# Local attention: epsilon by a sum over two columns, parameters read in place, W1 at the step's begin and the GELU of two items ahead of the output product

## The chip, the cores and the metric

The kernel runs on one core of a Trainium2 chip. The metric is the device time of one launch in microseconds. The core's engines are called PE (matrix products), DVE (vector), ACT (activations), POOL (the second vector engine) and SP (which issues the DMAs here); each runs its own list of instructions in order, and they meet through semaphores.

## The reference, cut to what matters

Input are 16 items of 256 tokens with 128 channels. Three parts follow one another: a first attention, six layers of local attention with a feed-forward part, and a state space part. The change is in the six layers:

```
for i in range(6):
    x = attn_layer(shift_tokens(x), Wqkv[i], q_scale[i], k_scale[i], Wo[i]) + x
    x = ffn_layer(shift_tokens(x), ln_g[i], ln_b[i], W1[i], b1[i], W2[i], b2[i]) + x

def ffn_layer(x, g, bln, W1, b1, W2, b2):
    mu = x.mean(-1, keepdims=True)
    var = ((x - mu) ** 2).mean(-1, keepdims=True)
    xn = (x - mu) / jnp.sqrt(var + 1e-05) * g + bln
    a, gate = jnp.split(xn @ W1 + b1, 2, -1)
    return a * jax.nn.gelu(gate, approximate=False) @ W2 + b2
```

`attn_layer` has 16 heads of 64, a norm and a rotation of q and k, and a softmax over the own window of 32 keys and the one before. The inner width of the feed-forward part is 341, kept in three chunks of 128, 128 and 85 rows, each with a value half (`ha`) and a gate half (`hgate`).

## The kernel before, in words

`phase_b` takes 96 items (6 layers of 16) through a pipeline written out in Python: `phase_b_steps` calls each engine's `body` for steps n = -1 to 98. In step n the *front* works on item n+1 (projection, rotation, norm of q and k), the *attention* on item n, the *tail* on item n-1 (product with Wo, residual, layer norm), the *ffn* stage on item n-2 (product with W1, GELU) and the *closing* stage on item n-3 (gate times value, product with W2, residual). Layer and item are plain Python numbers, so nothing is looked up at run time.

A step has 32 slots. They are no times: every engine walks through slots 0 to 31 in order, and tables say in which slot it issues what. The order within one engine is therefore fixed by the tables, and between engines by semaphores alone.

- Scores of the attention's four rounds: slots 0, 8, 16, 24 (PE L1007, L1018, then DVE's row maximum L1349). Exponentials (ACT L1177) four and five slots later, eight instructions a round. DVE scales them (L1339, L1343) seven and eight slots after the scores. PE turns them (L1029) and ACT copies the turned ones (L1220) at eight and eleven. Values (PE L1044) at fourteen, their copy (ACT L1208) at fifteen. What reaches past slot 31 is done in the next step.
- Scores wait until the exponentials of the round before have read the banks.
- Projection pieces (PE L1063 to L1065) at slots 0, 2, 6, 8, 15, 16, 17, 21, 22, 24, 29, 30, in two banks by turns. A piece waits until the piece two before it has been read: by DVE's rotation (L1291, L1293) for q and k, by ACT's copy (L1201) for v. Squares are ACT L1197, their sums DVE L1295; POOL adds the rotated halves (L1380), clamps (L1382) and takes the power (L1384). The norm's product is POOL's (L1369) or DVE's (L1302, slots 27 and, late, 4).
- Two *spare* PSUM banks go round by turns among: the turned q/k tiles (PE L992, ACT copy L1147; slots 24, 26, 27, 28 and, late, 0, 4, 6, 7), the product with Wo (L1081, slots 11 and 12), the turned residual `xt` (L1088, slot 21), the turned layer norm `xn` (L1094, slot 31; ACT's copy with scale and bias L1159), W1's three chunks (L1121) and W2 (L1108, slot 29; read by DVE L1326, slot 31). A use waits until the use two before it has been read (`take_spare`).
- W1's chunk c, at slot s of `W1_SLOT`: PE L1121, then ACT reads the two halves with their biases (L1166 into `hgate`, L1167 into `ha`). Slots: chunk 0 at 5, chunk 2 at 17, chunk 1 at 21.
- The GELU (ACT L1224) is taken in odd steps only, over the gates of two items at once (128x1536), at slot 21, after that slot's exponentials. It needs another activation table than the exponential. POOL multiplies gate and value at slot 19 (L1390) and waits for the GELU's semaphore.
- Layer norm, DVE, slot 22 (`centred_stats`, L270): statistics (L273), `memset` of `var` to epsilon (L276), aggregation (L278), subtraction of the mean (L281), variance plus epsilon (L282). POOL takes the power and scales, slot 23 (`scaled_pool`, L288, L291).
- At the begin of each step DVE copies parameters into small tiles: ln scale and bias (L1266, `lnp`), b2 (L1270, `lend`), b2 and b1 (L1278, `lp`). ACT waits for them (`lnp_ready`, `lp_ready`), DVE for `lp_ready` before L1326.
- In the last step before a layer and in its first one ACT and DVE convert the layer's projection weights, with four of the six conversions at slots 1, 4, 7 and 10.

Of the kernel before, what the change touches and what calls it, by code (L numbers as in the profile page):

```python
# [726 lines left out]
W1_SLOT = {5: 0, 17: 2, 21: 1}  # L727
# [10 lines left out]
GELU_SLOT, RSTD_SLOT, GATE_SLOT = 21, 23, 19  # L738
# [99 lines left out]
def phase_b(nc, g, d, ps):  # L838
    with ExitStack() as stack:
# [389 lines left out]
        def _(dve):  # L1229
            for buffer in (s.xhi, s.xlo):  # L1230
                nc.vector.memset(buffer[:].bitcast(F32), 0.0)
            for buffer in (s.xs2, s.ha, s.V):
# [17 lines left out]
            def body(step):  # L1250
# [6 lines left out]
                def known(value):  # L1257
                    return value if isinstance(value, int) else dve.snap(value)

                if step.front is not None:  # L1260
                    lf = known(step.front[0])
                    next_src = known((step.front[1] + 1) % NB * NT)
                if step.tail is not None:
                    lt, dst = known(step.tail[0]), known(step.tail[1] * NT)
                    x_lower, x_upper, x_all = g.xT[lower, bass.ds(dst, NT)], g.xT[upper, bass.ds(dst, NT - 1)], g.xT[:, bass.ds(dst, NT)]
                    nc.vector.tensor_scalar_mul(s.lnp[:, step.odd], g.lparam[:, bass.ds(lt, 1), 0:2].rearrange("p a k -> p (a k)"), 1.0).then_inc(s.lnp_ready, 1)  # L1266
                if step.closing is not None:
                    lw, end = known(step.closing[0]), known(step.closing[1] * NT)
# [2 lines left out]
                    if step.ffn is None:
                        kept.then_inc(s.lp_ready, 1)
                if step.ffn is not None:
                    lu = known(step.ffn[0])
# [597 lines left out]
```

## Time and profile before

| | us |
|---|---|
| median of 3 runs | 4741.89 (4740.1 to 4744.51) |
| profiled execution | 4741.16 |
| its span, first to last instruction | 4739.4 |
| mean granted PE clock in it | 0.964 |
| local attention (`phase_b`) | some 500 to 4020 us of the span |

Times in the rows below are from the span's start. In timelines the first column is the start, the second the duration in us (merged over xN like instructions), and the bracket at the end is the idle time of the engine before it and who ended that. `b_`, `all_` and `until_b_` in front of a tile's name tell where it was allocated.

### The profile page before, as it was taken

The page shows a single profiled execution, that of the slowest core. Times are in us where ns is not written, and L with a number is a line of the kernel's source. Part 1 is how long each engine was busy: PE and PEld are TensorE (multiplying, and loading weights), DVE is VectorE, ACT ScalarE, POOL GpSimd, SP SyncE. Part 2 cuts the span into 40 slices and gives each one's busy share as a digit, 9 for nine tenths or more (in the row PEclk, how much of TensorE's full clock was granted, in tenths as well). Part 3 has the DMA queues.
Part 4 walks back from the last instruction along what each step waited for, and adds up shares of the span by engine and source line. Part 5 has one row for each costly group of instructions (what it writes and reads, how often), then busy time and mean ns, then how long its engine had stood idle before and what let it go on. Part 6 is the DMA issues. An engine that isn't in the chain of part 4 may idle for free. (4 is left out here: it accounts for less than half of the span.)

```text
span 4739.4 us, 124337 instructions
## 1 busy us (share of the span) xinstructions
PE 4228.0 (89%) x45166; PEld 3156.2 (67%) x45166; DVE 4078.0 (86%) x7658; ACT 3755.3 (79%) x11543; POOL 3540.7 (75%) x2504
## 2 busy tenths in 40 slices
PE   6898699999999999999999999999999997688887
PEld 3555477777777777777777777777777775445453
DVE  4776798989999999999999899999999995598887
ACT  2555588888888888888888888888888886777774
POOL 0010698999999899999999999999899994444444
PEclk9999799999999999999999999999999999788888
DMA  1000111112111121111111112111111111000000
GB/s 26 7 6 2 47 51 38 45 40 57 53 39 45 43 54 48 44 44 45 52 47 45 42 47 53 46 45 39 51 50 42 45 39 31 0 4 3 3 3 5
DMA packets 118569, 168.67 MB, mean 36 GB/s; under 512 B 26563, under 2 KB 44422, under 8 KB 118022
## 3 DMA queue, kind: packets, MB, share of 16 engines
q1 hardware_dynamic: 109246, 160.92, 12.8%
q8 instruction: 344, 5.64, 0.5%
q10 hardware_dynamic: 8776, 0.45, 0.1%
q14 instruction: 203, 1.66, 0.1%
HBM read 20.79 MB, written 2.10 MB: 5 GB/s over the span
## 5 line engine op out<-in xcount | busy, mean ns | idle before, releaser
L1380 POOL TENSOR_TENSOR b_w<-b_w,b_vt 128x512 f32<-128x512 f32 x768 | 1171.2, 1535 | 255.3 <-DVE b_vt L1293 145.3
L1384 POOL TENSOR_TENSOR b_rn<-b_ssm,all_neg_half 128x16 f32<-128x16 f32 x384 | 1219.2, 3175 | 32.0
L1177 ACT ACTIVATE b_Pr<-ps,b_nm 128x96 f32<-128x96 f32 x3072 | 1003.3, 354 | 0.6
L1177 ACT ACTIVATION_READ_ACCUMULATOR b_Pr<-ps,b_nm 128x1 f32 x3072 | 679.0, 221 | 0.0
L1220 ACT ACTIVATE b_PT<-ps 96x512 f32<-96x512 f32 x768 | 456.9, 595 | 240.3 <-PE ps L1029 227.4
L1063 PE MATMUL ps<-b_Whi,b_xlo 128*128 128x512 f32 x1152 | 579.5, 503 | 33.4 <-DVE b_vt L1293 18.5
L992 PE MATMUL ps<-all_ident,b_w 128*128 128x128 f32 x3072 | 467.9, 284 | 156.0 <-ACT b_qkT L1147 100.4
L1291 DVE TENSOR_TENSOR b_w<-ps,until_b_rotab 128x512 f32<-128x512 f32 x768 | 524.6, 683 | 60.5 <-ACT b_sq L1197 57.5
L1343 DVE TENSOR_TENSOR b_Pr<-b_Pr,b_rinv 128x384 f32<-128x384 f32 x768 | 534.7, 696 | 26.3
L1293 DVE TENSOR_TENSOR b_vt<-ps,until_b_rotab 128x512 f32<-128x512 f32 x768 | 523.0, 681 | 0.0
L1147 ACT ACTIVATE b_qkT<-ps 128x512 f32<-128x512 f32 x768 | 460.5, 613 | 76.6 <-PE ps L992 76.4
L1295 DVE TENSOR_REDUCE b_ss<-b_sq 128x8 f32<-128x512 f32 x768 | 519.5, 676 | 0.0
L1197 ACT ACTIVATE b_sq<-ps 128x512 f32<-128x512 f32 x768 | 476.0, 620 | 28.1 <-PE ps L1065 13.0
L1029 PE MATMUL ps<-all_ident,b_Pr 128*96 128x128 f32 x3072 | 478.5, 279 | 21.8 <-DVE b_Pr L1343 5.8
L992 PEld LDWEIGHTS ps<-all_ident,b_w 128*128 128x128 f32 x3072 | 343.6, 143 | 206.8 <-ACT b_qkT L1147 111.5
L1044 PEld LDWEIGHTS ps<-b_PT,b_V 96*64 96x64 f32 x12288 | 389.4, 138 | 137.4 <-issue 135.2
L1065 PE MATMUL ps<-b_Whi,b_xhi 128*128 128x512 f32 x1152 | 458.7, 398 | 0.0
L1064 PE MATMUL ps<-b_Wlo,b_xhi 128*128 128x512 f32 x1152 | 457.5, 397 | 0.0
L1044 PE MATMUL ps<-b_PT,b_V 96*64 96x64 f32 x12288 | 442.4, 225 | 1.2 <-ACT b_PT L1220 1.2
L1349 DVE TENSOR_REDUCE b_nm<-ps 128x8 f32<-128x768 f32 x384 | 367.5, 957 | 71.2 <-PE ps L1018 64.3
L1029 PEld LDWEIGHTS ps<-all_ident,b_Pr 128*96 128x96 f32 x3072 | 332.2, 127 | 121.5 <-issue 55.1
L1369 POOL TENSOR_TENSOR b_w<-b_w,b_rn 128x1024 f32<-128x1024 f32 x192 | 365.7, 1905 | 15.1
(259 smaller groups left out, 9461.0 us busy)
## 6 DMA issues: line engine op xcount, KB each, us to landing
b_V<-b_Vraw SPq DMA_DIRECT2D x384, 192.0 KB, 2.6
b_V<-b_Vraw SPq DMA_DIRECT2D x384, 128.0 KB, 2.4
b_V<-b_Vraw SPq DMA_DIRECT2D x192, 64.0 KB, 2.2
b_Wraw<-in_L_ffn_Wqkv SPq DMA_DIRECT2D x36, 256.0 KB, 3.4
b_Wo<-in_L_ffn_Wo SPq DMA_DIRECT2D x6, 512.0 KB, 4.1
a_xtok<-in_L_attn_hidden_states SPq DMA_DIRECT2D x16, 128.0 KB, 2.1
out<-c_xout SPq DMA_DIRECT2D x16, 128.0 KB, 1.8
b_W<-in_L_ffn_W SPq DMA_DIRECT2D x6, 341.0 KB, 3.7
```

Source lines behind the costliest of these rows:

```text
L992: last = nc.tensor.transpose(bank[:, i * P:(i + 1) * P], s.w[:, tt, c % 2, c // 2, i * P:(i + 1) * P], g.ident[:])
L1029: last = nc.tensor.transpose(ps[KEY_ROWS, T_BANK, (j * TT + tt) * P:(j * TT + tt + 1) * P], s.Pr[:, r % 2, j, a * TT + tt], g.ident[:])
L1044: last = nc.tensor.matmul(ps[j * DB:(j + 1) * DB, O_BANK, a * NT + blk * BLK:a * NT + (blk + 1) * BLK], s.V[KEY_ROWS, blk, head], s.PT[KEY ...
L1063: nc.tensor.matmul(ps[:, F_BANK[k % 2]], s.xlo[:, pf, rows], s.Whi[:, cols], start=True, stop=False)
L1177: last = nc.scalar.activation(s.Pr[:, r % 2, j, i], ps[:, S_BANK[j], i * KEYS:(i + 1) * KEYS], ACT.Exp, bias=s.nm[:, r, j, i:i + 1], accum ...
L1197: nc.scalar.activation(s.sq[:, i % 2], ps[:, F_BANK[k % 2]], ACT.Square).then_inc(s.act_front, 1)
L1291: nc.vector.tensor_tensor(s.w[:, tt, c % 2, which].rearrange("p (h e) -> p h e", e=DB), rotated, g.rotab[:, bass.ds(lf, 1), 2 * which, tt] ...
L1293: nc.vector.tensor_tensor(turned, raw[:, :, ::-1], sin.rearrange("p a (z e) -> p a z e", z=2).broadcast_to((P, 8, 2, DB // 2)), ALU.mult). ...
L1295: nc.vector.tensor_reduce(s.ss[:, j, which * 8:(which + 1) * 8], s.sq[:, i % 2].rearrange("p (h e) -> p h e", e=DB), AX.X, ALU.add).then_i ...
L1343: nc.vector.tensor_tensor(rows, rows, inverse, ALU.mult).then_inc(s.scaled, 1)
L1380: nc.gpsimd.tensor_tensor(rows, rows, s.vt[:, i % 4], ALU.add).then_inc(s.pool_add, 1)
L1384: nc.gpsimd.tensor_tensor(s.rn[:, j], s.ssm[:, j], g.neg_half[:, 0:HB], ALU.pow).then_inc(s.pool_r, 1)
```

## The change

Four edits, all in the local attention.

1. `ff`'s moment tile gets a third column that is set to epsilon once. Variance plus epsilon is a `tensor_reduce` over columns 1 and 2, in place of a `memset` and a `tensor_tensor`.
2. DVE's three parameter copies at the step's begin and their waits go; ACT and DVE read `g.lparam` in place.
3. W1's chunks 0, 1, 2 are at slots 1, 3, 5. The order of uses of the two spare banks follows from the slots, 15 uses a step as before.
4. The GELU is at slot 10, after the exponentials of slot 5 and before those of slot 12.

`bass.ds` of a Python number becomes a plain slice in the rotation, which is the same access.

```diff
+class CentredNorm(LayerNorm):
+    def __init__(self, s, name, xn):
+        super().__init__(s, name, xn)
+        self.mv = s.sb(name + "_mve", [P, TT, 3])
...
     dve.wait_ge(ln.moment, 2 * n + 1)
-    nc.vector.memset(ln.var[:], LN_EPS)
     for tt in range(TT):
-        last = nc.vector.bn_aggr(ln.mv[:, tt], ln.st[:, tt])
+        last = nc.vector.bn_aggr(ln.mv[:, tt, 0:2], ln.st[:, tt])
...
-    nc.vector.tensor_tensor(ln.var[:], ln.mv[:, :, 1], ln.var[:], ALU.add).then_inc(ln.var_ready, 1)
+    nc.vector.tensor_reduce(ln.var[:], ln.mv[:, :, 1:3], AX.X, ALU.add).then_inc(ln.var_ready, 1)
...
-W1_SLOT = {5: 0, 17: 2, 21: 1}
+W1_SLOT = {1: 0, 3: 1, 5: 2}
...
-GELU_SLOT, RSTD_SLOT, GATE_SLOT = 21, 23, 19
+GELU_SLOT, RSTD_SLOT, GATE_SLOT = 10, 23, 19
...
-                        act.wait_ge(s.lnp_ready, t + 1)
-                        nc.scalar.activation(s.xnT[:], ps[:, SPARE[bank], 0:NT], ACT.Identity, bias=s.lnp[:, pa, 1:2],
-                                             scale=s.lnp[:, pa, 0:1]).then_inc(s.spare_free[bank], 1)
+                        nc.scalar.activation(s.xnT[:], ps[:, SPARE[bank], 0:NT], ACT.Identity, bias=g.lparam[:, step.tail[0], 1:2],
+                                             scale=g.lparam[:, step.tail[0], 0:1]).then_inc(s.spare_free[bank], 1)
...
-                        act.wait_ge(s.lp_ready, u + 1)
...
+            nc.vector.memset(s.ff.mv[:], LN_EPS)
...
-                    nc.vector.tensor_scalar_mul(s.lnp[:, step.odd], g.lparam[:, bass.ds(lt, 1), 0:2].rearrange("p a k -> p (a k)"), 1.0).then_inc(s.lnp_ready, 1)
...
-                    kept = nc.vector.tensor_scalar_mul(s.lend[:], g.lparam[:, bass.ds(lw, 1), 2:3].rearrange("p a k -> p (a k)"), 1.0)
...
-                    if ("w1", 0) in step.uses_before:
-                        for b, uses in step.latest([("w1", c) for c in range(3)], True):
-                            dve.wait_ge(s.spare_free[b], uses + 1)
-                    nc.vector.tensor_scalar_mul(s.lp[:], g.lparam[:, bass.ds(lu, 1), 2:9].rearrange("p a k -> p (a k)"), 1.0).then_inc(s.lp_ready, 1)
...
-                            dve.wait_ge(s.lp_ready, u + 1)
-                            nc.vector.scalar_tensor_tensor(out=x_end, in0=ps[:, SPARE[b], 0:NT], scalar=s.lend[:], in1=x_end,
+                            nc.vector.scalar_tensor_tensor(out=x_end, in0=ps[:, SPARE[b], 0:NT], scalar=g.lparam[:, lw, 2:3], in1=x_end,
```

## Rows read from the trace of the kernel before

**Rows 1.** Busy time by windows: us, then PE, PEld, DVE, ACT, POOL busy, PEclk, DMA.

```profile
600.00:3990.00 3390.00, 3150.01 (x38588) 2509.12 (x38580) 3094.75 (x6031) 2977.62 (x9863) 3078.13 (x1963) 0.99 0.17 46
```

**Rows 2.** Timeline of DVE, steps 35, 41 and 42 (cut).

```profile
1796.14 1.25 DVE L1266 TENSOR_SCALAR b_lnp<-until_b_lparam 128x2 f32<-128x2 f32 x1
...
1833.75 0.16 DVE L1266 TENSOR_SCALAR b_lnp<-until_b_lparam 128x2 f32<-128x2 f32 x1
...
2011.77 1.25 DVE L1266 TENSOR_SCALAR b_lnp<-until_b_lparam 128x2 f32<-128x2 f32 x1
...
2020.90 0.17 DVE L1339 RECIPROCAL b_rinv<-b_ssum 128x4 f32<-128x4 f32 x1
...
2030.43 0.96 DVE L1349 TENSOR_REDUCE b_nm<-ps 128x8 f32<-128x768 f32 x1
...
2036.03 0.96 DVE L282 TENSOR_TENSOR b_ff_var<-b_ff_mv,b_ff_var 128x2 f32<-128x2 f32 x1
...
2038.90 0.96 DVE L1349 TENSOR_REDUCE b_nm<-ps 128x8 f32<-128x768 f32 x1 [0.41 <-PE ps L1018]
...
2048.28 0.16 DVE L1266 TENSOR_SCALAR b_lnp<-until_b_lparam 128x2 f32<-128x2 f32 x1
...
2067.32 0.96 DVE L1349 TENSOR_REDUCE b_nm<-ps 128x8 f32<-128x768 f32 x1
...
2075.80 0.96 DVE L1349 TENSOR_REDUCE b_nm<-ps 128x8 f32<-128x768 f32 x1 [0.41 <-PE ps L1018]
...
2083.05 1.25 DVE L1266 TENSOR_SCALAR b_lnp<-until_b_lparam 128x2 f32<-128x2 f32 x1
```

**Rows 3.** Timeline of ACT, step 41 (cut).

```profile
2020.06 0.63 ACT L1197 ACTIVATE b_sq<-ps 128x512 f32<-128x512 f32 x1
...
2025.07 0.59 ACT L1220 ACTIVATE b_PT<-ps 96x512 f32<-96x512 f32 x1 [1.57 <-PE ps L1029]
...
2028.78 0.60 ACT L1201 ACTIVATE b_Vraw<-ps 128x512 f32<-128x512 f32 x1 [0.56 <-PE ps L1065]
...
2037.70 1.28 ACT L1224 ACT_TABLE_LOAD   x1
2039.00 1.49 ACT L1224 ACTIVATE b_hgate<-b_hgate 128x1536 f32<-128x1536 f32 x1
2040.39 0.58 ACT L1197 ACTIVATE b_sq<-ps 128x512 f32<-128x512 f32 x1
```

**Rows 4.** Timeline of PE, step 41 (cut).

```profile
2016.08 1.03 PE L1121 MATMUL ps<-b_xnT,b_W 128*128 128x256 f32 x4
...
2019.58 1.06 PE L992 MATMUL ps<-all_ident,b_w 128*128 128x128 f32 x8 [0.69 <-DVE b_w L1302]
...
2037.83 0.36 PE L1007 MATMUL ps<-until_b_mask_bf,until_b_ident_bf 64*64 64x384 bf16 x4 [0.44 <-ACT b_Pr L1177]
...
2042.49 0.66 PE L992 MATMUL ps<-all_ident,b_w 128*128 128x128 f32 x4 [2.18 <-ACT b_qkT L1147]
```

**Rows 5.** Windows of the first and the last of 15 half-clock stretches (PEclk 0.50).

```profile
744.70:748.10 3.40, 3.40 (x11) 2.76 (x9) 2.15 (x3) 3.37 (x10) 3.40 (x3) 0.50 0.00 0
3700.70:3704.00 3.30, 3.28 (x14) 3.14 (x15) 3.30 (x5) 2.54 (x5) 3.22 (x4) 0.50 0.01 2
```

**Rows 6.** Lines of DVE: count, duration ns min/median/max, first and last start us, shapes.

```profile
L1266 DVE TENSOR_SCALAR b_lnp<-until_b_lparam x96: 156/184/1257, 575.3 to 3989.2; 128x2 f32<-128x2 f32 x96
L282 DVE TENSOR_TENSOR b_ff_var<-b_ff_mv,b_ff_var x96: 150/956/1084, 598.4 to 4000.6; 128x2 f32<-128x2 f32 x96
L1295 DVE TENSOR_REDUCE b_ss<-b_sq x768: 667/676/682, 514.0 to 3953.5; 128x8 f32<-128x512 f32 x192
L1343 DVE TENSOR_TENSOR b_Pr<-b_Pr,b_rinv x768: 557/559/1681, 548.1 to 3990.0; 128x384 f32<-128x384 f32 x192
```

**Rows 7.** Timeline of POOL, additions at the step's begin and at L282.

```profile
2009.18 3.81 POOL L1380 TENSOR_TENSOR b_w<-b_w,b_vt 128x512 f32<-128x512 f32 x2
...
2034.45 2.52 POOL L1380 TENSOR_TENSOR b_w<-b_w,b_vt 128x512 f32<-128x512 f32 x2
```

More of the change, by code:

```diff
@@ L855, in phase_b @@
         s.oT = s.sb("oT", [P, HPAIRS, NT])
-        s.lp = s.sb("lp", [P, 7]); s.lend = s.sb("lend", [P, 1]); s.lnp = s.sb("lnp", [P, 2, 2])
         s.xs2 = s.sb("xs2", [P, NT]); s.xtok = s.sb("xtok", [P, TT, P]); s.xnT = s.sb("xnT", [P, NT])
         s.ha = s.sb("ha", [P, 2, 3, NT]); s.hgate = s.sb("hgate", [P, 2, 3, NT])
-        s.ff = LayerNorm(s, "ff", s.xtok)
+        s.ff = CentredNorm(s, "ff", s.xtok)
         s.zeroed, s.wo_in, s.w1_in, s.w2_in, s.whi_done, s.w_ready = s.sems("zeroed wo_in w1_in w2_in whi_done w_ready")
@@ L865, in phase_b @@
         s.pv_done, s.rinv_ready, s.scaled, s.ocopied = s.sems("pv_done rinv_ready scaled ocopied")
-        s.lp_ready, s.lnp_ready, s.shifted, s.gelu_done, s.hg_ready, s.x_ready = s.sems("lp_ready lnp_ready shifted gelu_done hg_ready x_ready")
+        s.shifted, s.gelu_done, s.hg_ready, s.x_ready = s.sems("shifted gelu_done hg_ready x_ready")
         s.wqkv_in = s.sems(" ".join(f"wqkv_in_{i}" for i in range(RAW)))
@@ L1163, in read_spare @@
                         width = FF_CHUNKS[c][1]
-                        act.wait_ge(s.lp_ready, u + 1)
+                        lu = step.ffn[0]
                         bank = full_spare(("w1", c))
-                        nc.scalar.activation(s.hgate[0:width, pa, c], ps[0:width, SPARE[bank], NT:2 * NT], ACT.Identity, bias=s.lp[0:width, 4 + c:5 + c])
+                        nc.scalar.activation(s.hgate[0:width, pa, c], ps[0:width, SPARE[bank], NT:2 * NT], ACT.Identity, bias=g.lparam[0:width, lu, 6 + c:7 + c])
                         nc.scalar.activation(s.ha[0:width, pa, c], ps[0:width, SPARE[bank], 0:NT], ACT.Identity,
-                                             bias=s.lp[0:width, 1 + c:2 + c]).then_inc(s.spare_free[bank], 1)
+                                             bias=g.lparam[0:width, lu, 3 + c:4 + c]).then_inc(s.spare_free[bank], 1)
                 def exps(item, r, a):
@@ L1255, in full_spare @@
                     dve.wait_ge(s.spare_full[bank], uses + 1)
-                def known(value):
-                    return value if isinstance(value, int) else dve.snap(value)
                 if step.front is not None:
-                    lf = known(step.front[0])
-                    next_src = known((step.front[1] + 1) % NB * NT)
+                    lf, next_src = step.front[0], (step.front[1] + 1) % NB * NT
                 if step.tail is not None:
-                    lt, dst = known(step.tail[0]), known(step.tail[1] * NT)
-                    x_lower, x_upper, x_all = g.xT[lower, bass.ds(dst, NT)], g.xT[upper, bass.ds(dst, NT - 1)], g.xT[:, bass.ds(dst, NT)]
-                    nc.vector.tensor_scalar_mul(s.lnp[:, step.odd], g.lparam[:, bass.ds(lt, 1), 0:2].rearrange("p a k -> p (a k)"), 1.0).then_inc(s.lnp_ready, 1)
+                    dst = step.tail[1] * NT
+                    x_lower, x_upper, x_all = g.xT[lower, dst:dst + NT], g.xT[upper, dst:dst + NT - 1], g.xT[:, dst:dst + NT]
                 if step.closing is not None:
-                    lw, end = known(step.closing[0]), known(step.closing[1] * NT)
-                    x_end = g.xT[:, bass.ds(end, NT)]
-                    kept = nc.vector.tensor_scalar_mul(s.lend[:], g.lparam[:, bass.ds(lw, 1), 2:3].rearrange("p a k -> p (a k)"), 1.0)
[L1271 to L1274, printed above, removed]
-                    if ("w1", 0) in step.uses_before:
-                        for b, uses in step.latest([("w1", c) for c in range(3)], True):
-                            dve.wait_ge(s.spare_free[b], uses + 1)
-                    nc.vector.tensor_scalar_mul(s.lp[:], g.lparam[:, bass.ds(lu, 1), 2:9].rearrange("p a k -> p (a k)"), 1.0).then_inc(s.lp_ready, 1)
+                    lw, end = step.closing[0], step.closing[1] * NT
+                    x_end = g.xT[:, end:end + NT]
                 def rotate(at):
@@ L1289, in rotate @@
                     turned = s.vt[:, i % 4].rearrange("p (h z e) -> p h z e", z=2, e=DB // 2)
-                    sin = g.rotab[:, bass.ds(lf, 1), 2 * which + 1, tt]
+                    sin = g.rotab[:, lf:lf + 1, 2 * which + 1, tt]
                     nc.vector.tensor_tensor(s.w[:, tt, c % 2, which].rearrange("p (h e) -> p h e", e=DB), rotated,
-                                            g.rotab[:, bass.ds(lf, 1), 2 * which, tt].broadcast_to((P, 8, DB)), ALU.mult)
+                                            g.rotab[:, lf:lf + 1, 2 * which, tt].broadcast_to((P, 8, DB)), ALU.mult)
                     nc.vector.tensor_tensor(turned, raw[:, :, ::-1], sin.rearrange("p a (z e) -> p a z e", z=2).broadcast_to((P, 8, 2, DB // 2)),
```

## The prediction

> **What bounds the kernel now.** I read the page first, then the busy time by windows, the waits of the middle of the run, and last the timelines of two neighbouring steps, engine by engine. The page names no single bound. In the 3,390 us that the local attention fills, PE is busy 93%, DVE 91%, POOL 91% and ACT 88% [rows 1]: four engines near full, so an instruction that goes away pays only where the others wait for its engine. The longest waits come once in two steps, in the odd step, which holds the GELU.
>
> The DVE timeline gives the steps their lengths [rows 2]. I call the four row maxima (L1349) of a step, slots 0, 8, 16 and 24, M0 to M3. Step 41 (odd) begins at 2011.77; the reader sees M2 18.66 us later, M3 8.47 after that, and the next step 9.38 after M3: 36.51. Step 42 (even): M2 at 19.04, M3 8.48 later, the end 7.25 later: 34.77. So the GELU costs the odd step about 2.1 us, between M3 and the end, and hands the even step a late start.
>
> What happens there: ACT loads the GELU table at 2037.70, and its next other instruction starts 2.69 us later, at 2040.39 [rows 3]; before the next exponentials the table changes back, one more such load of 1.28. PE stands for 2.18 us meanwhile, behind ACT's copy L1147 [rows 4]. In 15 of the odd steps PE's granted clock falls to 0.50 (1.2 GHz) for 3.4 us right behind this gap, the first near 745 us and the last near 3,701 [rows 5]. Such a step is 1.1 us longer than its like: step 35 goes from 1796.14 to 1833.75, 37.61 [rows 2].
>
> **The change, part by part.**
>
> *Copies at the step's begin, epsilon.* L1266 takes 0.16 to 1.25 us for 128x2 values, L282 mostly 0.96 [rows 6]. Both end with a POOL addition: L1266 of 2011.77 ends at 2013.02, POOL's pair at 2012.99; L282 of 2036.03 ends at 2036.99, POOL's pair at 2036.97 [rows 2, 7]. They wait for POOL, they don't work. With the two copies behind L1266 DVE is held 1.3 us. The reduce that replaces L282 reads one source; the nearest row is L1295, a reduce that stayed within 667 to 682 ns over 768 times whatever POOL did [rows 6]. For 128x2 outputs I take 0.15, L282's shortest; nothing is the lower bound. But behind both places stands L1343, with two SBUF inputs too, whose length goes from 0.56 to 1.68 [rows 6]: it inherits the wait. At the step's begin it would start at 2012.0, wait for POOL to 2012.99 and end near 2013.5; it now ends near 2013.8. So 0.3 of the 1.3 is left, and at L282 something like 0.2 of 0.8. Bounds: 0.5 and the full 2.1 us of DVE a step.
>
> The Trainium skill says the same of the port pair (SBUF — State Buffer, the two separate sides): a DVE operation with two SBUF inputs and a GpSimd operation that reads SBUF lock each other out for whole instructions. It is a rule against this half of the change, since the next such operation pays; the sum here goes by the rows.
>
> *W1 at slots 1, 3, 5 in place of 5, 17, 21.* Four matmuls (L1121 at 2016.08) take PE some 0.72 us [rows 4], two ACT reads 0.72 as well, at 0.36 from start to start. Two such sets come into slots 1 to 4. Before the transposes of slots 6 and 7 PE had 0.69 idle, until 2019.58, for DVE's L1302 [rows 4]; 1.44 us more work makes them 0.75 late. On ACT the square of slot 2 comes 0.8 late, behind PE's W1, which eats the 0.3 that DVE had won; the reads of slot 3 stand between it and the exponentials, which end about 1.6 us later than today. They now end as the square of slot 6 begins, 2020.06, and DVE's L1339 comes for them at 2020.90 [rows 2, 3]: 0.8 of slack, so M1 and M2 come about 0.85 later. PE and DVE agree: M2 at 18.66 + 0.85 = 19.51 in a step whose start is not disturbed, against 19.04 in today's even step. Bounds: nothing (18.66) and the full 1.5 us (20.2). The two alternate banks make PE wait for each ACT read before the next use but one; that is inside the 0.85.
>
> At slots 17 and 21 the same work goes. It pays little: PE's piece of slot 22 waits by the code for DVE's turn of slot 17 (L1293), and DVE is busy without a gap there, so DVE sets it, and W1 had filled PE's wait. What is won is the 0.44 us that PE waits for the exponentials before M3's scores [rows 4]; ACT, without two pairs of reads, is 1.4 us earlier. M2 to M3 becomes 8.48 - 0.44 = 8.04; M3 to the end stays at the undisturbed 7.25. Even step: 19.51 + 8.04 + 7.25 = 34.80, today 34.77: nothing.
>
> *GELU at slot 10 in place of 21.* It follows the copy of slot 8, which ends at 2023.50 (2025.07 less 1.57 idle [rows 3]), with the 0.75 of the late PE at 2024.25. The next copy starts 2.69 later, 2026.94. From that copy to the end of the eight exponentials it takes 3.15 us today (2025.07 to 2028.22, that is 2028.78 less 0.56 idle [rows 3]), with the exponential's table 4.43: 2031.37. The scores of round 2 wait for them, start 0.2 later, and M2 comes 1.07 after their start (2037.83 to 2038.90 [rows 2, 4]): 2032.64, 20.87 into the step. The GELU thus still costs 1.36 us over the even step; of its 4.0 on ACT, idle time (1.57 + 0.56 [rows 3]) and lag hide the rest. Queued behind it: the exponentials, PE's scores, the value copy of slot 15. POOL's product L1390 (slot 19) then finds the GELU long done; it didn't wait for it before either. Odd step: 20.87 + 8.04 + 7.25 = 36.16, today 36.51: 0.35 less. Bounds: fully hidden (34.8) and a stall of all 4.0 (38.8).
>
> The Trainium skill (ScalarE: Activation LUTs, what a table load costs) gives 1.28 us for the load and about 1.38 of drain beside it. The rows show the 1.28 and no drain: the GELU starts at 2039.00, 0.02 after its load ends [rows 3]. By the page the two loads would add 2.76 us before M2.
>
> *Clock.* PE's idle stretch before M2's scores becomes 1.3 to 1.4 us, in place of 2.18. Gaps of 0.69 were never followed by the half clock, those of 2.18 in 15 steps. I take it as gone: 1.35 is nearer to 0.69. 15 x 1.1 = 16.5 us.
>
> **Sum.** A pair of steps: 34.80 + 36.16 = 70.96 against 71.28, 0.32 less. 43 of the 48 pairs are such; in the five in which a layer's weights are converted ACT has four conversions more in slots 1 to 10, and I take nothing. 43 x 0.32 = 13.8; with the clock 30.3. The profiled execution took 4741.2 around a span of 4739.4; 4741.2 - 30.3 = 4710.9, and the median 4741.89 lies 0.7 above it: **4711 us**. Setup, the first attention and the state space part are untouched.
>
> **Rivals.**
> 1. *The early W1 is wholly on the path: slower.* Place: slots 1 to 5, PE and ACT handing two banks to and fro between scores and exponentials. M2 slips by 1.5, not 0.85, in both steps: a pair is 1.0 us longer than today, 43 of them +43, less the clock's 16.5: 4768. It decides once the slip is 0.35 us a step larger than mine. For it: 0.69 us of idle PE is less than the added work. Against: DVE is busy throughout and should pace.
> 2. *The stall only moves, half clock included.* GELU and table in front of M2 cost 1.7 us, and PE's gap there is long enough for the clock to fall: 4741, no change.
> 3. *The early W1 is hidden.* M2 at 18.66 (even) and 20.1 (odd): steps of 33.9 and 35.4, a pair 2.0 less: 4741.9 - 86 - 16.5 = 4639. PE's 93% of 35.9 us, 33.4 in a step, forbids much more.
> 4. *Each table change holds ACT longer than its load.* Both loads now stand in front of M2. If each held ACT a further load's length, 1.28 us, the odd step would be 2.56 - 0.35 = 2.2 us longer than today: 4741.9 + 95 = 4837. The skill's drain would do that, too; the 0.02 us behind the load is against it.
>
> **Chances.** Forecast 0.55, rival 1 0.17, rival 2 0.14, rival 3 0.12, rival 4 0.02. 0.2% (9.5 us) is about what a measurement of this kernel can tell from no change. Faster: 0.55 + 0.12 = 0.67; same: 0.14; slower: 0.17 + 0.02 = 0.19. The forecast's own range, a slip 0.3 us smaller or larger a step, is 4685 to 4737. To leave out no more than 2 in 10, the range takes in rival 2, most of the way to rival 1 and most of that to 3: 4650 to 4760.
>
> **What would show it.** DVE: no L1266, L1270, L1278, L276; L282's reduce under 0.2 us in every step; L1343's mean above today's, since it inherits. Odd step: M2 near +20.9, M3 8.0 later, the end 7.25 later; even step: M2 near +19.5. PE: a gap of some 1.4 us before round 2's scores in odd steps and none of 2.18; no granted clock of 0.50 between 1,000 and 3,700 us. Wrong if M2 slips by over 1.2 us in even steps, if the end after M3 is not 7.25, or if the clock still falls.

## The result, and the profile after

| | before | after |
|---|---|---|
| median, us | 4741.65 (4740.1 to 4744.51, 4 runs) | 4788.07 (4786.35 to 4790.56, 4 runs) |
| ratio, 95% interval | | 1.0098 [1.0085, 1.0111] |
| span of the profiled execution | 4739.4 | 4788.8 |

The change costs 46 us, 1.0%, where 4711 and a gain were forecast; the time is above the upper end of the range, 4760. The averages tell little. In the window of [rows 1] PE is as busy as before (3,151 us against 3,150), ACT 12 us less, POOL 33 and DVE 71 us less; PE does 458 matrix products fewer there, so the window just holds less of the work. The first row is that of the windows view (us, then PE, PEld, DVE, ACT, POOL busy, PEclk, DMA). The two under it are M0 to M1 of steps 41 and 42, and the second fence has the same two parts of the kernel before:

```profile
600.00:3990.00 3390.00, 3151.23 (x38130) 2470.57 (x38129) 3024.10 (x5609) 2965.67 (x9748) 3045.10 (x1952) 1.00 0.17 45
...
2030.00:2040.75 10.75, 10.70 (x120) 8.78 (x121) 9.04 (x16) 9.71 (x32) 9.33 (x5) 1.00 0.16 41
2066.94:2077.40 10.46, 10.40 (x119) 8.48 (x118) 9.05 (x17) 9.71 (x32) 9.58 (x5) 1.00 0.19 48
```

```profile
2013.77:2023.11 9.34, 8.53 (x109) 6.89 (x108) 9.18 (x18) 8.67 (x29) 8.78 (x5) 1.00 0.27 70
2050.66:2060.00 9.34, 8.89 (x111) 7.25 (x112) 9.18 (x17) 9.15 (x31) 5.92 (x4) 1.00 0.24 61
```

So the steps have to be laid side by side. L1266, from which the prediction counted, is gone; all lengths below go from row maximum to row maximum (now L1340), as in this timeline of DVE, the answer to [rows 2]:

```profile
2030.02 0.96 DVE L1340 TENSOR_REDUCE b_nm<-ps 128x8 f32<-128x768 f32 x1 [0.51 <-PE ps L1024]
...
2040.75 0.96 DVE L1340 TENSOR_REDUCE b_nm<-ps 128x8 f32<-128x768 f32 x1
...
2050.05 0.96 DVE L1340 TENSOR_REDUCE b_nm<-ps 128x8 f32<-128x768 f32 x1 [0.52 <-PE ps L1024]
...
2057.98 0.96 DVE L1340 TENSOR_REDUCE b_nm<-ps 128x8 f32<-128x768 f32 x1 [0.80 <-PE ps L1024]
...
2066.94 0.95 DVE L1340 TENSOR_REDUCE b_nm<-ps 128x8 f32<-128x768 f32 x1
...
2077.40 0.96 DVE L1340 TENSOR_REDUCE b_nm<-ps 128x8 f32<-128x768 f32 x1
...
2084.67 0.96 DVE L1340 TENSOR_REDUCE b_nm<-ps 128x8 f32<-128x768 f32 x1
...
2092.62 0.96 DVE L1340 TENSOR_REDUCE b_nm<-ps 128x8 f32<-128x768 f32 x1 [0.25 <-PE ps L1024]
...
2098.67 0.48 DVE L1317 SCALAR_TENSOR_TENSOR all_xT<-ps,until_b_lparam,all_xT 128x256 f32<-128x256 f32 x1 [0.39 <-PE ps L1114]
...
2100.54 1.44 DVE L1334 TENSOR_TENSOR b_Pr<-b_Pr,b_rinv 128x384 f32<-128x384 f32 x1
...
2102.49 0.96 DVE L1340 TENSOR_REDUCE b_nm<-ps 128x8 f32<-128x768 f32 x1 [0.51 <-PE ps L1024]
```

The first four rows are M0 to M3 of step 41 (odd), the next four those of step 42, the last is M0 of step 43. The differences, taken so over each run's profiled execution, have the medians below: some 40 odd and 40 even steps, without the five of each at the layers' edges. The four parts of a step are M0 to M1, M1 to M2, M2 to M3 and M3 to the next M0. "Half clock" counts the stretches with a PEclk of 0.50 between 650 and 3,950 us. The times are medians of the launches. The runs under the first two lines are the experiments, and the ratios are against the kernel before, run beside each.

| run | us | ratio [95%] | odd step: parts = whole | even step | half clock |
|---|---|---|---|---|---|
| before | 4741.65 | | 9.33 7.33 8.48 11.77 = 36.91 | 9.34 7.32 8.47 9.26 = 34.40 | 15 |
| after | 4788.07 | 1.0098 [1.0085, 1.0111] | 10.73 9.29 7.94 8.95 = 36.92 | 10.46 7.27 7.95 9.85 = 35.54 | 4 |
| e1 | 4741.96 | 1.0002 [0.9993, 1.0012] | 9.34 7.33 8.41 12.62 = 37.69 | 9.34 7.33 8.40 9.00 = 34.07 | 36 |
| e2 | 4787.49 | 1.0097 [1.0080, 1.0114] | 10.52 9.28 7.94 9.14 = 36.88 | 10.40 7.29 7.95 9.71 = 35.34 | 4 |
| e3 | 4777.69 | 1.0074 [1.0058, 1.0091] | 10.72 7.28 7.94 10.60 = 36.54 | 10.73 7.28 7.94 9.84 = 35.79 | 1 |
| e4 | 4763.88 | 1.0048 [1.0032, 1.0065] | 10.40 9.29 7.94 8.67 = 36.30 | 10.74 7.27 9.02 8.68 = 35.71 | 4 |
| f5 | 4748.0 | 1.0012 [1.0003, 1.0022] | 10.74 7.27 7.95 9.86 = 35.81 | 10.73 7.27 7.94 9.85 = 35.80 | 0 |
| f6 | 4765.86 | 1.0051 [1.0034, 1.0067] | 10.45 9.29 7.94 8.94 = 36.63 | 10.18 7.27 7.94 9.85 = 35.25 | 5 |
| f7 | 4727.84 | 0.9973 [0.9964, 0.9983] | 10.05 9.29 7.94 8.95 = 36.23 | 9.79 7.27 7.95 9.86 = 34.88 | 6 |
| f8 | 4710.59 | 0.9938 [0.9921, 0.9954] | 9.34 7.33 8.43 11.77 = 36.86 | 9.34 7.33 8.41 8.99 = 34.07 | 1 |
| g1 | 4725.35 | 0.9965 [0.9953, 0.9978] | 9.34 7.32 8.46 11.75 = 36.88 | 9.34 7.33 8.46 9.27 = 34.40 | 0 |
| g2 | 4685.4 | 0.9880 [0.9864, 0.9897] | 9.34 7.33 8.43 11.28 = 36.37 | 9.34 7.33 8.41 8.99 = 34.08 | 1 |
| g3 | 4740.19 | 0.9998 [0.9988, 1.0008] | 9.34 7.33 8.43 12.39 = 37.49 | 9.34 7.33 8.42 8.98 = 34.08 | 0 |
| g4 | 4737.49 | 0.9989 [0.9979, 0.9999] | 10.74 9.29 7.94 8.68 = 36.65 | 10.74 7.27 7.95 8.68 = 34.63 | 6 |

(A whole's median need not be the sum of the parts'.) Against before, the odd step loses 1.4 and 2.0 us ahead of M2 and wins 0.5 and 2.8 behind it: nothing in sum. The even step loses 1.1 and, behind M3, 0.6, and wins 0.5: 1.1 us longer.

Four readings say why. First PE. In M0 to M1 it is idle for 0.05 of 10.75 and 0.06 of 10.46 us and DVE for 1.7 and 1.4; before, PE was idle for 0.8 and 0.45 and DVE for 0.16 (windows above). So PE is now the full engine of this part, and DVE no longer is. M1 itself doesn't wait for PE, though: DVE's last idle time ahead of it ends with ACT's exponentials, behind which ACT has run without a gap since 2033.45, when it read W1's second chunk:

```profile
2038.56 0.18 DVE L1330 RECIPROCAL b_rinv<-b_ssum 128x4 f32<-128x4 f32 x1 [0.74 <-ACT b_Pr L1182]
```

So the extra time of M0 to M1 is PE's and ACT's together; f6 and f7 below weigh them. PE's timeline, the answer to [rows 4]:

```profile
2039.81 0.64 PE L1035 MATMUL ps<-all_ident,b_Pr 128*96 128x128 f32 x4
...
2044.77 1.15 PE L1050 MATMUL ps<-b_PT,b_V 96*64 96x64 f32 x32 [0.42 <-ACT b_PT L1225]
...
2048.98 0.36 PE L1013 MATMUL ps<-until_b_mask_bf,until_b_ident_bf 64*64 64x384 bf16 x4 [1.47 <-ACT b_Pr L1182]
...
2061.36 1.46 PE L1114 MATMUL ps<-b_ha,b_W 128*128 128x256 f32 x6
...
2097.10 1.53 PE L1114 MATMUL ps<-b_ha,b_W 128*128 128x256 f32 x6 [0.94 <-POOL b_ha L1381]
```

The stall of 2.18 became one of 1.47 ahead of round 2's scores, and in step 42 a new one stands before W2 (L1114): it waits for POOL's product of gate and value. In the view of waits between 1,000 and 3,400 us (total, times, longest) that comes once in each pair:

```profile
PE ps L1013 <- ACT b_Pr L1182: 45.0, 32, 1.5
PE ps L1114 <- POOL b_ha L1381: 28.1, 32, 0.9
```

Second POOL: its product in steps 41 and 42. It starts 1.29 us after M3 in the one and 2.51 after M3 in the other; in step 42 of the kernel before it was 1.52 (2077.32 against M3 at 2075.80 [rows 2]). POOL's clamp and DVE's scaling ahead of it are shown too, and last POOL's rows of before.

```profile
2059.27 1.84 POOL L1381 TENSOR_TENSOR b_ha<-b_ha,b_hgate 128x768 f32<-128x768 f32 x1
...
2091.24 0.56 POOL L1373 TENSOR_SCALAR b_ssm<-b_ss 128x16 f32<-128x16 f32 x1
...
2095.13 1.83 POOL L1381 TENSOR_TENSOR b_ha<-b_ha,b_hgate 128x768 f32<-128x768 f32 x1
```

```profile
2090.53 1.15 DVE L1334 TENSOR_TENSOR b_Pr<-b_Pr,b_rinv 128x384 f32<-128x384 f32 x1
```

```profile
2073.82 0.25 POOL L1382 TENSOR_SCALAR b_ssm<-b_ss 128x16 f32<-128x16 f32 x1
...
2077.32 1.83 POOL L1390 TENSOR_TENSOR b_ha<-b_ha,b_hgate 128x768 f32<-128x768 f32 x1
```

Third ACT, step 41, the answer to [rows 3]. The copy of slot 8 has no bracket: PE had finished at 2040.45 (above), but ACT was still at its queue. The table load begins 11.43 us after M0.

```profile
2040.29 0.66 ACT L1202 ACTIVATE b_sq<-ps 128x512 f32<-128x512 f32 x1
2040.76 0.67 ACT L1225 ACTIVATE b_PT<-ps 96x512 f32<-96x512 f32 x1
2041.45 1.28 ACT L1229 ACT_TABLE_LOAD   x1
2042.75 1.49 ACT L1229 ACTIVATE b_hgate<-b_hgate 128x1536 f32<-128x1536 f32 x1
2044.14 0.57 ACT L1225 ACTIVATE b_PT<-ps 96x512 f32<-96x512 f32 x1
```

Fourth, the lines of DVE, the answer to [rows 6] (count: duration min/median/max in ns):

```profile
L289 DVE TENSOR_REDUCE b_ff_var<-b_ff_mve x96: 145/146/149, 597.2 to 4046.3; 128x2 f32<-128x4 f32 x96
L1334 DVE TENSOR_TENSOR b_Pr<-b_Pr,b_rinv x768: 557/560/1981, 547.0 to 4032.6; 128x384 f32<-128x384 f32 x192
```

The epsilon's reduce never waits. L1334, which follows it, does instead, now up to 1,981 ns: in step 42 it takes 1.15 us at 2090.53, beside POOL's addition, and POOL's clamp behind that takes 0.56 in place of 0.25.

### The profile page after: what moved, and what is told of

Same layout as the page of the kernel before. It is cut to its first block and busy times, and to the rows that moved or that the text cites. A ratio compares the mean times of both kernels' runs of the same rounds, so it can differ in the third digit from the quotient of the medians.

```text
span 4788.8 us, 123479 instructions
## 1 busy us (share of the span) xinstructions
PE 4271.4 (89%) x45166; PEld 3151.2 (66%) x45166; DVE 4030.1 (84%) x7275; ACT 3776.5 (79%) x11543; POOL 3525.6 (74%) x2504
## 5 line engine op out<-in xcount | busy, mean ns | idle before, releaser
L1371 POOL TENSOR_TENSOR b_w<-b_w,b_vt 128x512 f32<-128x512 f32 x768 | 1138.4, 1490 | 316.2 <-DVE b_ss L1287 261.1
L1375 POOL TENSOR_TENSOR b_rn<-b_ssm,all_neg_half 128x16 f32<-128x16 f32 x384 | 1172.1, 3052 | 32.0
L1182 ACT ACTIVATION_READ_ACCUMULATOR b_Pr<-ps,b_nm 128x1 f32 x3072 | 689.3, 224 | 0.0
L1334 DVE TENSOR_TENSOR b_Pr<-b_Pr,b_rinv 128x384 f32<-128x384 f32 x768 | 587.5, 765 | 26.3
L1035 PE MATMUL ps<-all_ident,b_Pr 128*96 128x128 f32 x3072 | 473.6, 277 | 10.3 <-ACT b_PT L1225 2.3
L998 PE MATMUL ps<-all_ident,b_w 128*128 128x128 f32 x3072 | 451.8, 280 | 7.6 <-DVE b_w L1294 7.0
L1340 DVE TENSOR_REDUCE b_nm<-ps 128x8 f32<-128x768 f32 x384 | 367.3, 956 | 105.4 <-PE ps L1024 102.3
L1035 PEld LDWEIGHTS ps<-all_ident,b_Pr 128*96 128x96 f32 x3072 | 327.6, 126 | 108.8 <-issue 50.0
L998 PEld LDWEIGHTS ps<-all_ident,b_w 128*128 128x128 f32 x3072 | 333.9, 140 | 48.0 <-issue 8.1
```

Of the source, the lines that this page charges most:

```text
L998: last = nc.tensor.transpose(bank[:, i * P:(i + 1) * P], s.w[:, tt, c % 2, c // 2, i * P:(i + 1) * P], g.ident[:])
L1035: last = nc.tensor.transpose(ps[KEY_ROWS, T_BANK, (j * TT + tt) * P:(j * TT + tt + 1) * P], s.Pr[:, r % 2, j, a * TT + tt], g.ident[:])
L1182: last = nc.scalar.activation(s.Pr[:, r % 2, j, i], ps[:, S_BANK[j], i * KEYS:(i + 1) * KEYS], ACT.Exp, bias=s.nm[:, r, j, i:i + 1], accum ...
L1334: nc.vector.tensor_tensor(rows, rows, inverse, ALU.mult).then_inc(s.scaled, 1)
L1371: nc.gpsimd.tensor_tensor(rows, rows, s.vt[:, i % 4], ALU.add).then_inc(s.pool_add, 1)
L1375: nc.gpsimd.tensor_tensor(s.rn[:, j], s.ssm[:, j], g.neg_half[:, 0:HB], ALU.pow).then_inc(s.pool_r, 1)
```

## The experiments

The first four split the change. Each starts from the kernel after, except e2, which starts from the one before. (A diff shows the edit against the kernel that the run starts from, for e1 the edits that it takes back.)

**e1**, edits 1 and 2 alone:

```diff
-W1_SLOT = {1: 0, 3: 1, 5: 2}
+W1_SLOT = {5: 0, 17: 2, 21: 1}
-GELU_SLOT, RSTD_SLOT, GATE_SLOT = 10, 23, 19
+GELU_SLOT, RSTD_SLOT, GATE_SLOT = 21, 23, 19
```

> Edits 1 and 2 alone (epsilon by the reduce, parameters in place); W1 at 5, 17, 21 and the GELU at 21 as before. Theory A (ACT's crowded slots 1 to 10 and, in even steps, POOL's gate product in front of W2 cost the 46 us): no cost here, M0 to M1 9.3, M1 to M2 7.3, 4720 to 4742 us, the start of a step 0.3 us shorter. Theory B (DVE's freed waits are inherited and push POOL back, so these two edits do the harm): slower than 4750, the end of the even step from M3 to the next M0 at 9.8 in place of 9.26.

Measured: 4741.96, no change. Yet the even step became 0.33 shorter (0.26 of it behind M3, where the copies stood at the next step's begin, and 0.07 at the epsilon). The half clock took it back: 36 stretches in place of 15, which puts it into most odd steps and so into their median, 37.69. PE's timeline of one, behind the same gap as in [rows 4], then the window of the stretch:

```profile
2038.68 0.60 PE L998 MATMUL ps<-all_ident,b_w 128*128 128x128 f32 x4
2041.46 0.78 PE L998 MATMUL ps<-all_ident,b_w 128*128 128x128 f32 x4 [2.17 <-ACT b_qkT L1153]
2042.04 1.06 PE L1035 MATMUL ps<-all_ident,b_Pr 128*96 128x128 f32 x4
```

```profile
2041.40:2044.80 3.40, 3.34 (x15) 2.99 (x16) 3.40 (x5) 2.87 (x7) 3.32 (x4) 0.57 0.03 7
```

The four products of L1035 take 1.06 us here and 0.60 elsewhere.

**e2**, edits 3 and 4 alone: the kernel before with the two slot tables of the kernel after.

> The kernel before with the two slot edits alone (W1 at 1, 3, 5, GELU at 10); epsilon and the copies as before. Theory A: all of the loss is here, 4785 to 4815 us, since the 0.3 us of the copies per step come on top; odd step M0 to M2 near 20.0. Theory B: near 4742, even step's M3 to M0 at 9.3.

Measured: 4787.49. The whole loss lies in the slots, and on top of them edits 1 and 2 give nothing (4788.07). The even step shows why: from M1 to the end of its product of gate and value POOL takes 19.16 us here (median), as before the change (19.15), and 19.55 in the kernel after. There edits 1 and 2 hand POOL 0.4 us of waits, the clamp of 0.56 above for one.

**e3**, the GELU back in its place, W1 early:

```diff
-GELU_SLOT, RSTD_SLOT, GATE_SLOT = 10, 23, 19
+GELU_SLOT, RSTD_SLOT, GATE_SLOT = 21, 23, 19
```

> The changed kernel with the GELU back at slot 21, W1 at 1, 3, 5. It tells W1's move from the GELU's. Theory A, W1's part: M0 to M1 at 10.5 in both steps (9.3 before), M1 to M2 7.3, M2 to M3 7.9; the odd step's end is long again (M3 to M0 11.2 to 11.8), PE stands some 2 us there and the granted clock falls to 0.50 behind it in a part of the odd steps: 4770 to 4800 us, about as slow as the change. If the GELU's place is what costs: 4720 to 4745.

Measured: 4777.69. W1 alone costs 36 us against e1, and more at the same clock: e1 has 36 stretches of half clock and e3 one. Against f8 below, which is e1 without them, it is 67 us. And the GELU's move, which was to win, costs another 10 us (4788.07 - 4777.69). M1 to M2 falls from 9.29 to 7.28, and 10.60 behind M3, against 9.84 in the even step, is all that the GELU costs there: POOL's gate ends 4.32 us after M3 in both (medians), and the GELU's stall partly lies beside that wait. PE's stall behind the GELU is 1.01 in place of 2.17, and the half clock stays away; the 11.2 to 11.8 and the falls of the clock that were expected did not come.

**e4**, POOL's product of gate and value earlier:

```diff
-GELU_SLOT, RSTD_SLOT, GATE_SLOT = 10, 23, 19
+GELU_SLOT, RSTD_SLOT, GATE_SLOT = 10, 23, 17
```

> The changed kernel with POOL's product of gate and value issued at slot 17 in place of 19, so ahead of the addition and the power of the last q/k piece before it; with the GELU at slot 10 it can be. Theory A: PE no longer waits 0.94 us for it before W2 in even steps, M3 to M0 goes from 9.85 to about 9.0 there, 48 x 0.85 = 40 us less: 4745 to 4760. If POOL is the bound of the step as a whole, moving work within it gives nothing: 4780 to 4795.

Measured: 4763.88, 24 us less than after. Behind M3 the even step gives back 1.17 (9.85 to 8.68), and M2 to M3 takes 1.07 of it (7.95 to 9.02). DVE's and POOL's timelines ahead of that M3, at 2083.71:

```profile
2080.56 1.68 DVE L1334 TENSOR_TENSOR b_Pr<-b_Pr,b_rinv 128x384 f32<-128x384 f32 x1
2082.16 0.17 DVE L1330 RECIPROCAL b_rinv<-b_ssum 128x4 f32<-128x4 f32 x1
2082.36 1.42 DVE L1334 TENSOR_TENSOR b_Pr<-b_Pr,b_rinv 128x384 f32<-128x384 f32 x1
```

```profile
2078.76 1.83 POOL L1381 TENSOR_TENSOR b_ha<-b_ha,b_hgate 128x768 f32<-128x768 f32 x1
2080.55 2.82 POOL L1371 TENSOR_TENSOR b_w<-b_w,b_vt 128x512 f32<-128x512 f32 x2
```

The time is still above the 4745 to 4760 expected. POOL's two additions now run back to back, and each of DVE's two products ends 0.4 us behind the end of one of them (the second at 2083.78, against 2083.37). It is the lock of the Trainium skill (SBUF — State Buffer, who interferes with whom): a DVE instruction with two SBUF inputs waits out a GpSimd instruction that reads SBUF. The rows agree: 1.68 and 1.42 us against 0.56 alone.

**f5, f6, f7 and g4** price one suspect each, by leaving work of the kernel after out.

```diff
 # f5: the GELU and both table loads
-... ACT.Gelu ...
+... ACT.Identity ...
 # f6: ACT's reads of W1's chunks 0 and 1
+                        cut = 8 if c < 2 else NT
-... s.hgate[0:width, pa, c], ps[0:width, SPARE[bank], NT:2 * NT] ...
+... s.hgate[0:width, pa, c, 0:cut], ps[0:width, SPARE[bank], NT:NT + cut] ...
 # f7: PE's products for the same chunks
-... matmul(bank[0:width, half * NT:(half + 1) * NT], ..., s.xnT[:], ...)
+... matmul(bank[0:width, half * NT:half * NT + cut], ..., s.xnT[:, 0:cut], ...)
 # g4: POOL's product of gate and value
-... s.ha[:, 1 - step.odd], ... s.hgate[:, 1 - step.odd] ...
+... s.ha[:, 1 - step.odd, :, 0:8], ... s.hgate[:, 1 - step.odd, :, 0:8] ...
```

> The changed kernel with the GELU replaced by the identity function: the pass over 128x1536 stays at slot 10, both table loads go, the GELU itself is left out of the computation. Theory: the two loads (2.56 us) stand wholly on the path in front of M2 in odd steps, so M1 to M2 falls from 9.29 to about 7.3 there and a pair loses 2.0 to 2.5 us: 4675 to 4695. The table loads' share of the loss against the kernel before would then be larger than the loss itself. Rival: ACT catches up before the exponentials only in part because W1's reads have used its idle time; then M1 to M2 stays above 8.3 and the time above 4730.

Measured: 4748.0, far less of a gain than expected. (The launches spread from 4740.85 to 4750.98, and the profiled one, 4740.94, is at the lower end.) M1 to M2 did fall to 7.27, but 0.9 came back behind M3: without the GELU's wait the gate is late in the odd steps too. The wait before W2 doubles, to both steps of a pair (view of waits):

```profile
PE ps L1114 <- POOL b_ha L1381: 63.7, 65, 1.5
```

> The changed kernel with ACT's reads of W1's chunks 0 and 1 (slots 1 and 3) cut from 256 to 8 columns; PE's matmuls are full. It leaves out most of the two chunks' values. Theory that ACT's crowded slots make M1 late: M0 to M1 goes from 10.5 to 10.7 down to 9.6 or less, 4740 to 4760 us. Theory that PE's added matmuls do it: M0 to M1 stays above 10.2, over 4775.

Measured: 4765.86; 0.28 us less in M0 to M1 of every step, between the two outcomes expected.

> The changed kernel with PE's matmuls of W1's chunks 0 and 1 cut from 256 to 8 columns, the weight loads and ACT's reads full (they read what lies in the bank). It leaves out most of the two chunks' product. Theory ACT: M0 to M1 stays at 10.2 or more, over 4770 us. Theory PE: M0 to M1 falls to 9.6 or less, under 4760. If both fall by half, the two share it, since PE and ACT hand the banks to each other.

Measured: 4727.84; 0.68 less. W1 adds 1.4 us to M0 to M1 of the odd step and 1.1 to that of the even one; PE's products are the larger part of it, ACT's reads the smaller, and neither is the whole.

> The changed kernel with POOL's product of gate and value cut from 256 to 8 columns of each chunk; it leaves out most of the gating. It takes away what I hold to be late in even steps without moving anything. Theory: M3 to M0 in even steps from 9.85 to 8.9 or 9.0, no wait of PE for POOL before W2, M2 to M3 stays 7.95: 4735 to 4750 us. If POOL was not what held W2 and the step's end: M3 to M0 stays at 9.7 or more and the time above 4775.

Measured: 4737.49, 51 us less than after, and within 0.2% of before. The even step loses its 1.17 behind M3: W2 starts 3.38 us after M3 in place of 4.48, and its products take 1.46 in place of 1.53. It no longer waits (POOL's, then PE's timeline; M3 at 2072.77, the next M0 at 2081.44):

```profile
2075.28 0.23 POOL L1381 TENSOR_TENSOR b_ha<-b_ha,b_hgate 128x24 f32<-128x24 f32 x1
```

```profile
2076.15 1.46 PE L1114 MATMUL ps<-b_ha,b_W 128*128 128x256 f32 x6
```

**f8 and g1** fill PE's gap: nine products of a bf16 identity in odd steps, into rows that nobody reads, ahead of the turn of slot 27. f8 is e1 with them, g1 the kernel before with them.

```diff
+                    if step.front is not None and step.odd and slot == FILL_SLOT:
+                        for _ in range(FILL):
+                            nc.tensor.matmul(ps[KEYS:P, T_BANK, 0:MASK_COLS], g.ident_bf[:, KEYS:P], g.mask_bf[:, 0], start=True, stop=True, skip_group_check=True)
```

> The run with epsilon and parameters alone (W1 and GELU where they were), and in odd steps nine more bf16 matmuls of 384 columns on PE in front of the transpose of slot 27, written to rows of a bank that nobody reads. They fill some 1.4 of the 2.2 us in which PE stands behind the GELU there. Theory that the half clock behind this gap takes back what the two edits gave: no granted clock of 0.50 (36 such stretches of 3.4 us without the filling), the odd step at 36.6 in place of 37.7, 4700 to 4712 us. Rival, that the clock's fall costs nothing because PE isn't the bound there: 4736 to 4745.

> The kernel before with nothing changed but the nine filling matmuls in odd steps. If each of its 15 half-clock stretches costs 1.1 us: 16 us less, 4722 to 4728. Then filling (16) and the two edits (14) add up to the 31 us of the filled run with both. If the edits gave nothing by themselves, this run takes 4710, too.

Measured: f8 4710.59, 31 us less than e1; g1 4725.35, 16 us less than before. The half clock is gone but for one stretch in f8, near 3,949 us, and nothing else moved: g1's steps are those of before. PE's timeline in f8 has the products and behind them 0.61 of idle time in place of 2.17:

```profile
2027.38 1.64 PE L1105 MATMUL ps<-until_b_mask_bf,until_b_ident_bf 128*32 128x384 bf16 x9
2029.63 0.66 PE L999 MATMUL ps<-all_ident,b_w 128*128 128x128 f32 x4 [0.61 <-ACT b_qkT L1157]
```

So 15 stretches cost the kernel before 16 us, 1.1 each, and with the half clock away edits 1 and 2 are worth 4725.35 - 4710.59 = 14.8 us, 0.31 a pair of steps, nearly all of it in the even one.

**g2** shortens the gap instead of filling it. It is e1 in which, in odd steps, DVE copies slot 24's turned tile, behind the row maximum, so that PE doesn't wait for ACT's GELU with it:

```diff
-                    if step.front is not None and at in TRANSPOSE_SLOT:
+                    if step.front is not None and at in TRANSPOSE_SLOT and not (step.odd and at in DVE_COPY_SLOT):
...
+                    if step.front is not None and step.odd and slot in DVE_COPY_SLOT:
+                        ...
+                        nc.vector.tensor_copy(s.qkT[:, 1 - step.odd, c * 4:c * 4 + 4, tt * P:(tt + 1) * P],
+                                              ps[:, SPARE[b]].rearrange("p (c t) -> p c t", c=4)).then_inc(s.spare_free[b], 1)
```

> Epsilon and parameters as in the change, W1 and GELU as before, and in odd steps the copy of the tile turned at slot 24 goes from ACT to DVE, which stands idle there behind the GELU. PE need not wait for ACT to free that bank: its gap of 2.2 us breaks in two, the half clock does not come (0 to 5 stretches), and ACT has 0.5 us less between GELU and exponentials: odd step 36.1 in place of 37.7, 4685 to 4705 us. Rival: the clock falls all the same behind a 1.4 us gap one transpose later, 4715 to 4735.

Measured: **4685.4, 1.2% under the kernel before** [0.9864, 0.9897] and 2.1% under the one after. The gap falls into two of 0.20 and 1.40, the half clock stays away (one stretch, near 3,925 us), and the odd step is 0.5 shorter than f8's. Of the 56 us under the kernel before, 15 are edits 1 and 2, 16 the half clock (g1), and 25 come with the copy (4710.59 - 4685.4). PE's and DVE's timelines:

```profile
2016.04 0.66 PE L999 MATMUL ps<-all_ident,b_w 128*128 128x128 f32 x4 [0.20 <-DVE b_qkT L1347]
2018.09 0.61 PE L1036 MATMUL ps<-all_ident,b_Pr 128*96 128x128 f32 x4 [1.40 <-ACT b_PT L1226]
```

```profile
2014.42 0.96 DVE L1341 TENSOR_REDUCE b_nm<-ps 128x8 f32<-128x768 f32 x1 [0.41 <-PE ps L1025]
2015.30 0.68 DVE L1347 COPY b_qkT<-ps 128x512 f32<-128x512 f32 x1
```

**g3** is g2 with six such filling products, at slot 28 (`FILL_SLOT, FILL = 28, 6`).

> The same with six filling matmuls in front of the transpose of slot 28 in odd steps. If the shorter gaps already keep the clock up: the same time as without them within 5 us. If not: 20 to 30 us less than without.

Measured: 4740.19, neither of the outcomes expected: the products stand behind the gap, not in it. PE waits its 1.40 first and then does 1.15 us that the turns behind it have to wait for; the odd step grows by 1.12.

```profile
2041.71 0.61 PE L1037 MATMUL ps<-all_ident,b_Pr 128*96 128x128 f32 x4 [1.40 <-ACT b_PT L1230]
2042.26 1.15 PE L1106 MATMUL ps<-until_b_mask_bf,until_b_ident_bf 128*32 128x384 bf16 x6
```

## Why the prediction was wrong, point by point

The prediction's step began some 1.7 us ahead of M0 (that DVE had won 0.3 there is in it). Counted from M0 it said: to M2 19.2 (odd) and 17.8 (even), to M3 8.04, to the next M0 8.95.

| | forecast | measured |
|---|---|---|
| odd, M0 to M2 | 19.2 | 20.02 |
| even, M0 to M2 | 17.8 | 17.73 |
| M2 to M3 | 8.04 | 7.94 |
| odd, M3 to M0 | 8.95 | 8.95 |
| even, M3 to M0 | 8.95 | **9.85** |
| pair | 70.96 | 72.46 |

**The step that failed: "M3 to the end stays at the undisturbed 7.25", in the even step.** It is 0.90 longer. M0 to M2 and M2 to M3 had been worked out for PE, DVE and ACT; of POOL the prediction said only that L1390 doesn't wait for the GELU. But POOL, too, has a queue, and nothing was taken out of it: additions, clamps, powers and norm products stand in a row before the gate's product. There was no slack to lose: before, the gate ended at 2079.15 in step 42, and W2 started at 2079.29. From M1 to M3 the step became 0.6 us shorter (15.80 to 15.22), and from M1 to the gate's end POOL became 0.4 longer (19.15 to 19.56), which is the share of edits 1 and 2 (19.16 in e2). So the gate ends 4.34 us after M3 in place of 3.35, W2 waits 0.94 for it, and DVE's L1317 behind that 0.39. PE sets the end of this step: DVE, whose L1334 of 1.44 us stands beside a POOL addition there, still waits 0.51 for PE's scores. g4 shows it from one side (POOL's product short: the 1.17 and 51 us come back), e4 from the other, f5 by the same wait in the odd steps once the GELU no longer holds them.

**The second: the GELU's 20.87, too small by 0.8.** Its table load comes 11.43 after M0 where 10.8 was forecast. The parts: about 0.3 is M0 itself, earlier against PE than in even steps, where DVE is the late one (M0 to M1 10.73 against 10.46, while PE's scores of rounds 0 and 1 lie 9.92 apart in both); 0.3 is ACT, which copied slot 8's tile when its queue allowed it, not when PE had it ready; 0.1 is the copy itself, 0.67 in place of 0.59. The forecast had moved PE's lateness on and left ACT the idle time of [rows 3], though W1's reads now fill it. Behind the load it took 8.60 to M2 where the forecast had 8.39.

**The sum.** 1.50 us a pair over the forecast, times 43, is 64.5: 4711 + 64.5 = 4775.5. The five pairs at the layers' edges, taken at nothing, grew by 1.74 each (40.11 + 34.94 to 40.26 + 36.53): 8.7, together 4784.2, of a measured 4788.07. The 3.9 left over are the balance of larger terms that the prediction had at nothing. In the profiled executions the stretch from M0 of step 95, the last one, to the last residual grew from 59.1 to 66.6 us, and the state space part behind it from 720.9 to 723.8 (it lies between 720.7 and 725.4 in all fourteen runs); what is ahead of the first M0 became 1.1 shorter. Against that the steps themselves took 2.7 less than 43 and five times these differences, and the profiled execution lies 2.5 above the median. Why the last step grew by 7.5 no run tells. (The forecast's own sum gives 4711.6, not 4711.) The four stretches of half clock that stayed are at the layers' edges, one behind a PE gap of 3.98 us, so their cost is in the 8.7 already.

**What held.** The clock's price (15 x 1.1; g1 has 16). The slip of early W1 (even step within 0.1), the 0.44 won ahead of M3 (0.53), the odd step's end, PE's gap of 1.3 to 1.4 (1.47) with no half clock behind it outside the layers' edges, L289 under 0.2 us, L1334 inheriting the wait (its mean goes from 696 to 765 ns). The copies and the epsilon, however, are worth 0.31 a pair of steps, not 0.3 a step and 0.2 more at the epsilon. L1266 takes 1.25 us in 45 of its 96 times only, at the begin of odd steps, as its median of 184 ns in [rows 6] says; the prediction took the 1.3 for every step. The instructions that went took 171 us more than the reduce in their place, 1.8 a step, and L1334 took 81 of them back in e1 (mean 696 to 802 ns, 768 times).

**The rivals.** Rival 1 (W1 wholly on the path, 4768) is nearest in time but has the wrong place: M0 to M2 of the even step is as forecast. e3, with 36 us lost by W1 alone (67 at the same clock), shows that it is W1 all the same that costs the time: the slip ahead of M1, which the forecast had, and the gate behind M3, which it hadn't. Rival 2 and rival 3 fell. Rival 4 fell by its own row: the GELU starts 0.02 us after its load, and behind the second load, at 2044.73, the exponentials go on at once. The Trainium skill's drain of some 1.38 us beside each load (ScalarE: Activation LUTs, what a table load costs) doesn't show in these rows either: 0.02 us ahead of each load and 0.02 behind it.

What stays open: why the half clock follows the same gap of 2.17 us in 36 odd steps of e1 and in 15 of the kernel before; no run told this apart.

## What to carry to other kernels

When work is moved ahead or a part of a step gets shorter, redo the sum for every engine's queue, those too from which nothing was taken: the one with no slack left sets the new wait, and a shorter M1 to M3 was no gain while POOL's row got no shorter. A gain in time can be paid back in clock, so compare the granted clock before calling an edit worthless (e1 alone looked like nothing and was worth 15 us, and e3 looked 36 us slower than e1 and is 67 at the same clock). And an edit's worth depends on which engine is the late one: edits 1 and 2 gave 15 us beside the old slots and nothing beside the new ones. Here a stall of two engines was cheaper to cut by giving one instruction to a third (g2, one copy of 0.68 us, 25 us won) than by moving the long instruction.

## What the runs showed of the hardware

- PE's granted clock fell from full (2.4 GHz) to 0.50 (1.2 GHz) for 3.4 us at a gap of 2.17 us in an otherwise full pipeline, in 15 odd steps of the kernel before and in 36 of e1, and cost 0.9 to 1.1 us each time (31 us over 35, 16 over 15). Nine products that compute nothing, 1.64 us of PE in such a gap, bought 16 us (g1) and 31 us (f8). Six of them behind a gap cost 55 us (g3 against g2). Gaps of 1.40 (g2) and 1.47 us (after) were not followed by it away from the layers' edges.
- Taking 1.8 us a step of DVE instructions away, most of it waits for POOL, gave 0.15 a step: the next instruction with two SBUF inputs waits for the same addition (L1334's mean 696 to 802 ns in e1). The wait goes the other way, too: POOL's clamp takes 0.56 us in place of 0.25 beside DVE's product (step 42). The reduce with one source ran in 145 to 149 ns 96 times out of 96.
